# GpSimd rounds x, new orders for 14 tiles, and another end for the last tile

## What is computed

```python
mask = adj > 0
head = mask / sqrt(sum(mask * mask, axis=-1))     # per row: mask / sqrt(count)
inc = adj + head
edge_fea = inc @ x
edge_degree = sum(inc, axis=-1)
y = x + edge_fea / edge_degree
out = (y - mean(y)) / sqrt(var(y) + 1e-5)          # over the 256 columns
```

## Time and profile before

| | us |
|---|---|
| median of 3 runs | 413.46 (413.26 to 413.9) |
| profiled execution, time | 412.91 |
| profiled execution, span of its instructions | 411.1 |
| PE busy | 390.0 (95%) |
| PEld busy | 342.5 (83%) |
| ACT busy | 373.6 (91%) |
| DVE busy | 361.5 (88%) |
| POOL busy | 343.7 (84%) |
| mean granted TensorE clock | 0.999 |

### The profile page before, as it was taken

The page is one execution under the profiler, slowest core; times in us unless marked ns, Lnnn a source line. Parts: engine busy times, 40 slices in busy tenths (PEclk is TensorE's granted clock), DMA queues, the critical chain, the costliest instruction groups (busy, mean ns, idle before and its releaser), DMA issues.

```text
span 411.1 us, 8801 instructions
## 1 busy us (share of the span) xinstructions
PE 390.0 (95%) x2216; PEld 342.5 (83%) x2216; DVE 361.5 (88%) x750; ACT 373.6 (91%) x512; POOL 343.7 (84%) x214
## 2 busy tenths in 40 slices
PE   0789999999999999999999999999999999999994
PEld 0778888788888888888888888888888888888884
DVE  0799798999999999999999999999999999999922
ACT  4975999999999999999999999999999999998421
POOL 2210589898999999999999999999999999999960
PEclk9999999999999999999999999999999999999999
DMA  8999996776767766677666666777676666670010
GB/s 232 259 235 257 269 266 171 219 219 183 229 193 209 212 204 192 211 215 217 195 211 202 197 205 192 205 214 219 197 213 197 198 209 185 208 211 26 26 53 26
DMA packets 36178, 79.94 MB, mean 194 GB/s; under 512 B 9536, under 2 KB 17728, under 8 KB 36160
## 3 DMA queue, kind: packets, MB, share of 16 engines
q1 hardware_dynamic: 35776, 78.68, 66.7%
q10 hardware_dynamic: 384, 1.05, 0.9%
HBM read 75.50 MB, written 4.19 MB: 194 GB/s over the span
## 4 chain that ended last, share of the span: by engine, by line
PE 53%; ACT 6%; issue 5%; DVE 4%; POOL 1%; DMA 1%; SPq 0%; POOLq 0%; ACTq 0%; DVEq 0%
PE edge L1124 32%; PE edge L1133 17%; PE edge L1075 4%; ACT scaled L246 2%; DVE inc L671 2%; ACT inc_split L257 2%; ACT sign_out L235 2%; DVE incT L687 1%; POOL inc_split L516 1%; PE sums L1070 1%; DMA raw<-in_adj_dram 1%; ACT rows L266 0%; SPq L154 0%; POOL small L500 0%; DVE rows L719 0%
## 5 line engine op out<-in xcount | busy, mean ns | idle before, releaser
L516 POOL TENSOR_TENSOR inc_split<-incT,inc_split 128x960 fp32r<-128x960 f32 x120 | 269.2, 2267 | 5.3 <-ACT inc_split L257 2.1
L1124 PE MATMUL edge<-x_split,inc_split 128*128 128x512 f32 (+1 forms) x930 | 222.4, 392 | 0.9 <-ACT inc_split L257 0.9
L1124 PEld LDWEIGHTS edge<-x_split,inc_split 128*128 128x128 f32 x930 | 168.0, 188 | 34.7 <-ACT inc_split L257 2.7
L671 DVE SCALAR_TENSOR_TENSOR inc<-raw,scaled 128x1024 f32<-128x1024 f32 x128 | 154.5, 1208 | 4.9 <-ACT scaled L246 4.4
L687 DVE STREAM_TRANSPOSE incT<-inc 128x1024 f32<-128x1024 f32 x128 | 156.3, 1230 | 0.7
L246 ACT ACTIVATE scaled<-raw,small 128x1024 f32<-128x1024 f32 x128 | 141.2, 1106 | 4.8 <-POOL small L535 3.3
L235 ACT ACTIVATE sign_out<-raw 128x1024 int8<-128x1024 f32 x128 | 133.6, 1045 | 1.3 <-DMA raw<-in_adj_dram 1.3
L1133 PEld LDWEIGHTS edge<-x_split,inc_split 128*128 128x128 f32 x900 | 112.0, 191 | 2.4
L1133 PE MATMUL edge<-x_split,inc_split 128*128 128x256 f32 x900 | 113.1, 283 | 0.0
L257 ACT CAST inc_split<-incT 128x960 fp32r<-128x960 f32 x90 | 86.2, 983 | 0.3 <-DVE incT L687 0.2
L535 POOL TENSOR_TENSOR small<-small 128x1 f32<-128x1 f32 x16 | 8.8, 552 | 38.6 <-DVE small L653 38.6
(11 more groups left out here) (37 smaller groups left out, 136.3 us busy)
## 6 DMA issues: line engine op xcount, KB each, us to landing
raw<-in_adj_dram SPq DMA_DIRECT2D x504, 128.0 KB, 2.6
rows<-in_x_dram SPq DMA_DIRECT2D x32, 128.0 KB, 2.1
out_dram<-rows SPq DMA_DIRECT2D x32, 128.0 KB, 1.7
x_stage<-in_x_dram SPq DMA_DIRECT2D x12, 256.0 KB, 10.4
raw<-in_adj_dram ACTq DMA_DIRECT2D x8, 128.0 KB, 5.2
x_stage<-in_x_dram SPq DMA_DIRECT2D x4, 192.0 KB, 14.6
x_native<-in_x_dram SPq DMA_DIRECT2D x4, 64.0 KB, 5.9
```

The source lines that it names most:

```text
L516: nc.gpsimd.tensor_tensor(lo_of(s, q), incT[:, s, 0:SPLIT, q, :], hi_of(s, q).bitcast(fp32), ALU.subtract).then_inc(lo_by_pool, 1)
L671: nc.vector.scalar_tensor_tensor(inc[:, q, :], raw[:, s, q, :], 0.0, scaled[q % 2][:, :], ALU.is_gt, ALU.add, accum_out=part_sums[:, s, 0, ...
L1124: last = nc.tensor.matmul(edge[s][:, c0:c1], inc_split[s][:, 0, b, :, :].rearrange("p q j -> p (q j)"), x_split[:, b, :, :].rearrange("p h ...
```

## The change

Three things are changed.

1. `split_x_hi` moves from ScalarE's list to GpSimd's, as a multiplication by 1.0 that writes the rounded type. `split_x_lo` on VectorE waits for GpSimd's semaphore in place of ScalarE's.
2. The calls of tiles 0 to 13 stand in other orders on ScalarE, GpSimd, VectorE and TensorE; the written-out part now reaches tile 13, and the loops begin at pair 7. On SP's queue the loads keep their order.
3. The last tile ends otherwise. Its 30 lo products go to the other bank, so that `y_last` adds the two halves of its own bank while they run, and the third part behind them. VectorE writes the result itself (`normalise_last`), in place of `shift_of` on VectorE and `normalise` on ScalarE. The shifts of tiles 29 and 30 and the rstd of tiles 28 and 29 stand earlier.

The diff, cut to its core (the orders of tiles 0 to 13 are shown further down where the prediction speaks of them):

```diff
@@ sync
-            for t in range(TILES - 2, TILES):
-                store(t, t % 2)
+            store(TILES - 2, 0)
+            sp.wait_ge(last_ready, 1)
+            sp.dma_start(out_rows[TILES - 1], y[:, 1, :]).then_inc(stored[1], 16)
@@ scalar
-            def split_x_hi(c):
-
-                act.wait_ge(x_in[c], FOUR_DMAS)
-                nc.scalar.copy(x_part(c, 0), x_staged(c)).then_inc(x_hi_by_act, 1)
...
-            split_x_hi(0)
             scale_early(1, 3)
-            split_x_hi(1)
-            split_x_hi(2)
-            split_x_hi(3)
...
-            with act.Fori(5, PAIRS - 2) as u:
+            with act.Fori(7, PAIRS - 2) as u:
...
-            normalise(31, 1)
@@ gpsimd
+            def split_x_hi(c):
+                pool.wait_ge(x_in[c], FOUR_DMAS)
+                nc.gpsimd.tensor_scalar(x_part(c, 0), x_staged(c), 1.0, 1.0,
+                                        ALU.mult, ALU.mult).then_inc(x_hi_by_pool, 1)
...
             norm_early(1, 3)
+            split_x_hi(0)
+            split_x_hi(1)
+            split_x_hi(2)
+            split_x_hi(3)
             norm_early(2, 0)
...
             round_quarter(31, 1, 1)
+            rstd_of(29, 1)
             low_quarter(31, 1, 1)
             low_quarter(31, 1, 2)
             low_quarter(31, 1, 3)
-            rstd_of(29, 1)
@@ vector
-                dve.wait_ge(x_hi_by_act, c + 1)
+                dve.wait_ge(x_hi_by_pool, c + 1)
...
+            def y_last(t, s, u):
+
+                dve.wait_ge(hi_used, t - FIRST_SPLIT + 1)
+                dve.wait_ge(xres_in[s], 16 * (u + 1))
+                dve.wait_ge(stored[s], 16 * u)
+                after(t, 2)
+                step(nc.vector.scalar_tensor_tensor(y[:, s, :], edge[s][:, D:2 * D], rdeg[:, :], xres,
+                                                    ALU.mult, ALU.add))
+                after(t, 3)
+                nc.vector.scalar_tensor_tensor(y[:, s, :], edge[s][:, 0:D], rdeg[:, :], y[:, s, :],
+                                               ALU.mult, ALU.add).then_inc(last_part, 1)
+                dve.wait_ge(edge_ready, t + 1)
+                dve.wait_ge(last_part, 1)
+                nc.vector.scalar_tensor_tensor(y[:, s, :], edge[1 - s][:, 0:D], rdeg[:, :], y[:, s, :],
+                                               ALU.mult, ALU.add).then_inc(y_ready, 1)
+
+            def normalise_last(t, s, u):
+                dve.wait_ge(rstd_ready, 4)
+                dve.wait_ge(stored[s], 16 * u)
+                nc.vector.tensor_scalar(y[:, s, :], y[:, s, :], mean_var[:, s, 0:1], norm_rstd[:, s, G:G + 1],
+                                        ALU.subtract, ALU.mult).then_inc(last_ready, 1)
...
             split_x_lo(0)
             split_x_lo(1)
+            degree(0, 0)
             split_x_lo(2)
             split_x_lo(3)
             count_early(2, 0)
-            degree(0, 0)
             count_early(2, 1)
...
-            shift_of(29, 1, alone=2)
+            shift_of(30, 0, alone=3)
             degree(31, 1)
             inverse_degree(31, 1)
-            y_first(31, 1, 15)
-            y_second(31, 1)
+            y_last(31, 1, 15)
             statistics(31, 1)
             mean_variance(31, 1)
             variance_eps(31, 1)
-            shift_of(30, 0, alone=3)
-            shift_of(31, 1, alone=4)
+            normalise_last(31, 1, 15)
@@ tensor
                 pe.wait_ge(lo_by_pool, G * t_split + G)
+                lo_out = edge[s][:, D:2 * D]
+                if last_tile:
+
+                    pe.wait_ge(y_ready, t)
+                    lo_out = edge[1 - s][:, 0:D]
```

More of the change, by code:

```diff
@@ L788, in _ @@
             inc_quarter(2, 0, 2)
+            statistics(0, 0)
+            count_early(3, 0)
             transpose_quarter(2, 0, 2, slot_split=False)
-            count_early(3, 0)
             inc_quarter(2, 0, 3)
@@ L915, in _ @@
             shift_of(6, 0)
+            variance_eps(7, 1)
             transpose_quarter(9, 1, 3)
-            variance_eps(7, 1)
-            with dve.Fori(5, PAIRS - 2) as u:
+            degree(8, 0)
+            inverse_degree(8, 0)
+            inc_quarter(10, 0, 0)
+            inc_quarter(10, 0, 1)
+            y_first(8, 0, 4)
+            transpose_quarter(10, 0, 0)
+            y_second(8, 0)
+            inc_quarter(10, 0, 2)
+            statistics(8, 0)
+            mean_variance(8, 0)
@@ new lines, in _ @@
+            count_of(11, 1)
+            transpose_quarter(10, 0, 1)
+            inc_quarter(10, 0, 3)
+            variance_eps(8, 0)
+            shift_of(7, 1)
+            degree(9, 1)
+            transpose_quarter(10, 0, 2)
+            transpose_quarter(10, 0, 3)
+            inc_quarter(11, 1, 0)
+            transpose_quarter(11, 1, 0)
+            inverse_degree(9, 1)
+            y_first(9, 1, 4)
+            inc_quarter(11, 1, 1)
+            y_second(9, 1)
+            statistics(9, 1)
@@ new lines, in _ @@
+            count_of(12, 0)
+            mean_variance(9, 1)
+            transpose_quarter(11, 1, 1)
+            inc_quarter(11, 1, 2)
+            shift_of(8, 0)
+            variance_eps(9, 1)
+            inc_quarter(11, 1, 3)
+            transpose_quarter(11, 1, 2)
+            transpose_quarter(11, 1, 3)
+            inc_quarter(12, 0, 0)
+            inc_quarter(12, 0, 1)
+            transpose_quarter(12, 0, 0)
+            degree(10, 0)
+            transpose_quarter(12, 0, 1)
+            inverse_degree(10, 0)
@@ new lines, in _ @@
+            y_first(10, 0, 5)
+            count_of(13, 1)
+            inc_quarter(12, 0, 2)
+            y_second(10, 0)
+            inc_quarter(12, 0, 3)
+            transpose_quarter(12, 0, 2)
+            shift_of(9, 1)
+            statistics(10, 0)
+            inc_quarter(13, 1, 0)
+            transpose_quarter(12, 0, 3)
+            mean_variance(10, 0)
+            inc_quarter(13, 1, 1)
+            variance_eps(10, 0)
+            degree(11, 1)
+            inverse_degree(11, 1)
+            transpose_quarter(13, 1, 0)
@@ L919, in _ @@
+            transpose_quarter(13, 1, 1)
+            y_first(11, 1, 5)
+            inc_quarter(13, 1, 2)
+            y_second(11, 1)
+            count_of(14, 0)
+            statistics(11, 1)
+            mean_variance(11, 1)
+            variance_eps(11, 1)
+            inc_quarter(13, 1, 3)
+            shift_of(10, 0)
+            transpose_quarter(13, 1, 2)
+            transpose_quarter(13, 1, 3)
+            with dve.Fori(7, PAIRS - 2) as u:
                 inc_quarter(2 * u, 0, 0)
@@ L1019, in _ @@
             shift_of(28, 0, alone=1)
+            shift_of(29, 1, alone=2)
             degree(30, 0)
@@ L1157, in _ @@
             warm_up()
+            warm_up()
+            warm_up()
             sum_early(1, 1)
+            warm_up()
             warm_up()
@@ L1188, in _ @@
+            tile(11, 1, {("hi", 11): lambda: sum_quadrants(11, 1)})
+            tile(12, 0, {("hi", 18): lambda: sum_quadrants(12, 0)})
+            tile(13, 1, {("hi", 12): lambda: sum_quadrants(13, 1)})
             SUMS_AT = ("hi", 12)
-            with pe.Fori(5, PAIRS - 1) as u:
+            with pe.Fori(7, PAIRS - 1) as u:
                 for s in range(2):
@@ L1194, in _ @@
                 t = TILES - 2 + s
-                tile(t, s, {SUMS_AT: lambda: sum_quadrants(t, s, signs=False)})
+                tile(t, s, {SUMS_AT: lambda: sum_quadrants(t, s, signs=False)}, last_tile=(s == 1))
 _INS = ["x", "adj"]
```

288 lines of the change are left out of this document (180 added, 108 removed).

## The result

The changed kernel took 415.52 us in the median of six runs (415.11 to 416.2), the kernel before, on the same chip, 413.49 (413.26 to 413.9). The ratio is 1.0042, with a 95% interval of 1.0029 to 1.0055: by the medians 2.0 us slower, where 1.85 was forecast (the medians' own ratio, 1.0049, lies inside the interval). The profiled run of the changed kernel took 415.57 us with a span of 413.8; the earlier trace rows belong to a span of 411.1.

The account below looks back on a forecast made before the run. ScalarE was taken to set the pace from 41 us to tile 10, then TensorE, with DMA bounding before. 2.9 - 0.1 - 0.95 = +1.85 gave 415.3 us for the median; range 414.4 to 415.9, or 412.3 to 415.9 with both large cases.

Parts of the forecast that it names:

- Casts leave ScalarE: Before tile 2: taking 7.2 us of casts from ScalarE gains 0, because it waits for DMA there.
- Casts and subtractions in turn: Ahead of tile 2: GpSimd's casts and VectorE's subtractions alternate, holding ScalarE about +2.9 us (2.3 to 3.6).
- The block: VectorE's four subtractions for x's second part before tile 2, 8.32 us; forecast to end at 44.0 instead of 40.62.
- The cover of 0.45 us: Ahead of tile 2's first scaling: the subtractions may end 0.45 us later without delaying ScalarE.
- two of the signs: Trace marks of a right forecast, among them tile 2's first scaling at 44 to 45 us, tile 11's first product near 165.8.
- The choice between the ends: Casts beside subtractions: side by side (lower end) or in turn (upper end, +2.9 us); upper taken as little more likely than not.
- TensorE's start: At the head: later products delay tile 0's degree sum; costs 0 with casts in turn, a 0.5 us hold side by side.
- New orders: Tiles 2 to 13: the reordered calls bring -0.1 us (-0.3 to +0.5), as ScalarE has no idle time in either order.
- The rival of new waits: Tiles 3 to 13: late VectorE passes hold ScalarE's scalings, one microsecond in all, casts hidden; 413.5 to 414.5 us, chance 0.10.
- the first case: Casts and subtractions in turn ahead of tile 2: 414.4 to 415.9 us, chance 0.50.
- Tail: Last tile: one addition fewer after the last product and one VectorE result pass, -0.95 us (-0.9 to -1.15).
- A delay of ScalarE is handed on one to one: After 41 us: any delay of ScalarE delays tile 10, the loop and the end by the same amount.

Follow-up runs that it names:

- cast_only: The kernel before with only the four casts moved from ScalarE to GpSimd; +2.04 us, ratio 1.0027 to 1.0062.
- degree_late: The changed kernel with tile 0's degree pass put back behind the four subtractions, casts on GpSimd; +1.81 us against the kernel before.
- casts_back: The changed kernel with the casts back on ScalarE, tile 0's degree pass left early; +0.76 us against the kernel before.
- casts_back_degree_late: The changed kernel with casts back on ScalarE and tile 0's degree pass behind the subtractions, leaving new orders and tail; +0.68 us against the kernel before.
- tail_only: The kernel before with only the new end of the last tile; -0.74 us, ratio 0.9964 to 0.9997.
- sign10: The changed kernel with one ScalarE pair restored, tile 9's first scaling ahead of tile 10's second signs; +0.69 us against the kernel before.
- tail_norm_acc: As tail_norm_dve, but each of the seven passes also writes a sum (accum_out); 1.65 us faster than the kernel before, ratio 0.9949 to 0.9980.
- tail_norm_dve: The kernel before with the new tail and tiles 0 to 6's results written by VectorE in one pass; 5.9 us slower, ratio 1.0139 to 1.0190.

## Why the prediction was right, point by point

- **Casts leave ScalarE: 0.** Right. The signs of tile 2 still wait for DMA (38.46, 11.30 us idle before).
- **Casts and subtractions in turn: +2.9.** The mechanism is right and shown by three kernels; the size was 1.72. The block was forecast to end at 44.0 and ended at 42.82. Of the 1.18, 0.34 is the start (31.26, not 31.6); 0.36 the casts (2.14 and 1.60 were scaled from 960 elements as if a pass had no fixed part; 2048 take 1.90, and the line through 960 and 2048 gives 1.48 for 1536); 0.36 the handovers, of which the trace shows none; 0.1 stands in no one row. The cover of 0.45 us was right: 2.20 late at the block's end, 1.72 at the scaling. With the size two of the signs failed: the scaling wasn't at 44 to 45 but at 43.56, and tile 11's first product at 164.9, not near 165.8. In cast_only, where the block starts at 32.23, the hold is 2.4.
- **The choice between the ends.** The argument that decided it, an unfamiliar kind of pass with little cover, held. The Trainium skill, SBUF — State Buffer, section "Who interferes with whom", had this rule, and the traces now agree: 11.28 us in place of 8.32 beside reading passes, 8.32 beside memsets. The same section of the Trainium skill says that one-source passes take turns with GpSimd when they run in a mode that uses both interfaces, and that a form that also writes out its accumulator can't enter it. No row shows the mode of a pass; the times, 1.70 us in the mean without the sum and 0.53 with it, agree.
- **TensorE's start: 0 beside the casts, 0.5 without.** degree_late shows the first (at most 0.3), casts_back the second (0.4). Chunk 18 was late by more than walked (35.45, not 34.1) because of the clock, and this cost nothing.
- **New orders: -0.1.** This step failed. "ScalarE has no idle time in either order, so it can't come out ahead" is true and misses what matters: an order also decides what stands between a late load and the pass that needs it. casts_back_degree_late shows 1.9 us lost after tile 8 with next to no hold, and 1.4 in its median against tail_only; sign10 shows one of the places. The range ended at +0.5. The rival of new waits, one microsecond, had the size but blamed late VectorE passes; the waits were for `raw` in the main, and the sum of the first case had no room for them.
- **Tail: -0.95.** Right: -0.96 and -0.97 in the two traces.
- **A delay of ScalarE is handed on one to one.** Right: +2.42 at tile 2 and +2.45 at tile 31 in cast_only. The premise that ScalarE alone sets that pace isn't borne out: a delay of ScalarE counts in full, but in tail_norm_acc work taken from it and given to VectorE gained almost nothing.

The total was right partly by luck: the hold was 1.2 us too large, and the orders' losses, which I had at a gain of 0.1, were 1.7 in the profiled run and filled the place.

## What to carry to other kernels

Before moving a pass from ScalarE to GpSimd, list VectorE's passes that run at the same time and read SBUF through two operands or, like the result pass of tail_norm_dve, in a one-operand form without a sum: here they took turns with GpSimd's passes that read SBUF, whole pass for whole pass. An engine that is idle in the profile isn't free if it shares what it reads through. When passes are reordered, look also at what stands between a load and its first user; a microsecond of other work there is cover that no busy share shows.

## What the runs showed of the hardware

- A pass that waits for the shared reading is shown as busy. In the changed kernel the third cast is 2.50 us long with no idle time in it, about 0.6 of it waiting. Only its length against its like (1.90) tells.
- VectorE's 256-element pass with two small scalars takes 0.41 us where GpSimd is idle (the tail) and up to 2.40 beside its subtractions.
- Loads of the program's code take time on the DMA engines that move the data (5.1% from 123.5 to 125 us in the changed kernel): pieces of 128 KB beside them land after 3.2 to 5.0 us in place of 2.5.
- The granted clock from 25 to 30 us was 0.66 in the changed kernel and in degree_late, and 1.00 in casts_back_degree_late, with the same idle time ahead of the first sum (1.98, 1.97 and 1.96 us). It was 0.66 in all four traces that have the new head with the casts on GpSimd, and 1.00 in both that have it with the casts on ScalarE. What decides it stays open.
